# A five-layer transformer stack on one core: GpSimd takes the rounding of a layer's products, a pair of masked keys and a broadcast, and every engine gets a new order

## The reference, cut to what matters

```python
t = t + L2_attn(_ln_t(t))   # 8 heads of 16, causal window of 64
t = t + L2_ffn(_ln_t(t))    # the quantized product, below
t = t + L3_attn(_ln_t(t))   # 8 heads of 16, causal
t = t + L3_ffn(_ln_t(t))    # router, 8 experts of 128x512x128, top 2

def _L2_ffn_ref(x, weight, bias):
    ...
    y = jnp.dot(x, effective_weight) + bias
    act_clipped = jnp.clip(y, -1.0, 1.0)
    quant_dequant = jnp.round(act_clipped * 7.0) / 7.0
    return _ste(y, quant_dequant)      # y + (quant_dequant - y)
```

## Time and profile before

| | |
|---|---|
| median of 3 runs | 240.2 us (240.07 to 240.32) |
| the profiled execution | 240.61 us, span 238.8 us |
| TensorE busy | 227.2 us (95%) |
| VectorE busy | 203.1 us (85%) |
| ScalarE busy | 170.0 us (71%) |
| GpSimd busy | 89.6 us (38%), 155 instructions |
| granted TensorE clock | 0.999 |

### The profile page before, as it was taken

The page is one execution under the profiler, slowest core; times in us unless marked ns, Lnnn a source line. Parts: engine busy times, 40 slices in busy tenths (PEclk is TensorE's granted clock), DMA queues, the critical chain, the costliest instruction groups (busy, mean ns, idle before and its releaser), DMA issues.

```text
span 238.8 us, 4613 instructions
## 1 busy us (share of the span) xinstructions
PE 227.2 (95%) x1493; PEld 172.8 (72%) x1493; DVE 203.1 (85%) x524; ACT 170.0 (71%) x500; POOL 89.6 (38%) x155
## 2 busy tenths in 40 slices
PE   7999999899999999998999979999999999999993
PEld 2588566567876667575876657888888888888882
DVE  2768888975899989999999776999999985899885
ACT  2276454699869986989879968667658766666560
POOL 6200124888864857276733888121100000000000
PEclk9999999999999999999999999999999999999999
DMA  6910000002300200020000333211110004512001
GB/s 187 346 58 4 0 0 0 1 3 88 92 0 5 88 3 0 0 86 6 3 1 0 90 92 96 82 47 44 45 44 0 3 0 116 151 53 78 5 1 44
DMA packets 9319, 11.71 MB, mean 49 GB/s; under 512 B 704, under 2 KB 5952, under 8 KB 9168
## 3 DMA queue, kind: packets, MB, share of 16 engines
q1 hardware_dynamic: 8864, 11.09, 15.4%
q10 hardware_dynamic: 432, 0.33, 0.4%
HBM read 10.87 MB, written 0.56 MB: 48 GB/s over the span
## 4 chain that ended last, share of the span: by engine, by line
PE 76%; DVE 11%; ACT 7%; issue 2%; DMA 1%; POOL 0%; SPq 0%; DVEq 0%; ACTq 0%
PE bank L1317 6%; PE bank L1329 6%; PE bank L1319 6%; PE bank L1318 6%; PE bank L1332 6%; PE bank L1330 6%; PE bank L948 6%; PE bank L924 5%; ACT early_prob L583 4%; PE bank L971 3%; PE bank L882 3%; PE bank L893 2%; ACT prob L583 2%; PE bank L930 2%; PE bank L995 2%
## 5 line engine op out<-in xcount | busy, mean ns | idle before, releaser
L811 ACT ACTIVATE hb<-bank,pk 128x512 f32<-128x512 f32 x64 | 42.9, 705 | 20.7 <-PE bank L1319 20.7
L1818 DVE TENSOR_TENSOR hlo<-hb,hhi 128x512 fp32r<-128x512 f32 x64 | 43.8, 707 | 5.8 <-ACT hhi L814 4.6
L1457 DVE TENSOR_REDUCE negmax<-bank 128x2 f32<-128x384 f32 (+2 forms) x48 | 29.5, 639 | 4.9 <-PE bank L930 4.8
L583 ACT ACTIVATE prob<-bank,negmax 128x192 f32<-128x192 f32 (+1 forms) x64 | 28.9, 508 | 5.1 <-DVE negmax L1457 5.1
L539 ACT ACTIVATE probT<-bank 128x512 f32<-128x512 f32 x38 | 23.1, 638 | 3.4 <-PE bank L948 2.1
L1317 PE MATMUL bank<-xhi,w_hi 128*128 128x512 f32 x64 | 25.3, 396 | 0.0
L1329 PE MATMUL bank<-hhi,w_hi 128*128 128x512 f32 x64 | 25.1, 392 | 0.0
L1319 PE MATMUL bank<-xhi,w_lo 128*128 128x512 f32 x64 | 25.0, 390 | 0.0
L1318 PE MATMUL bank<-xlo,w_hi 128*128 128x512 f32 x64 | 24.9, 390 | 0.0
L1332 PE MATMUL bank<-hlo,w_hi 128*128 128x512 f32 x64 | 24.9, 389 | 0.0
L1330 PE MATMUL bank<-hhi,w_lo 128*128 128x512 f32 x64 | 24.9, 389 | 0.0
(11 more groups left out here) (156 smaller groups left out, 525.9 us busy)
## 6 DMA issues: line engine op xcount, KB each, us to landing
w_raw<-w SPq DMA_DIRECT2D x16, 256.0 KB, 3.1
comb_b<-routes SPq DMA_DIRECT2D x16, 256.0 KB, 3.3
pk<-packed SPq DMA_DIRECT2D x1, 1280.0 KB, 8.9
pk<-packed SPq DMA_DIRECT2D x1, 560.0 KB, 5.9
xs<-x SPq DMA_DIRECT2D x3, 128.0 KB, 2.9
out<-acc SPq DMA_DIRECT2D x3, 128.0 KB, 1.7
xs<-x ACTq DMA_DIRECT2D x1, 128.0 KB, 3.2
out<-acc ACTq DMA_DIRECT2D x1, 128.0 KB, 1.7
```

The lines of the kernel that those rows point to most:

```text
L583: last = nc.scalar.activation(prob_of(n, u)[:, of], lane[n][u % 2][:, of], ACT.Exp, bias=negmax[n][:, unit_query(u), h:h + 1], accum_out=s ...
L811: nc.scalar.activation(hb[blk % 2][:, j, :], h_bank[j][:, :], ACT.Relu, bias=bias).then_inc(h_ready, 1)
L1457: V.tensor_reduce(negmax[n][:, unit_query(u), heads[0]:heads[-1] + 1], lane[n][u % 2][:, :].rearrange("q (h k) -> q h k", h=len(heads))[:, ...
L1818: V.tensor_tensor(hlo[blk % 2][:, j, :], hb[blk % 2][:, j, :], hhi[blk % 2][:, j, :].bitcast(F32), ALU.subtract).then_inc(hlo_ready, 1)
```

## The change

Three pieces of work go from VectorE to GpSimd, with semaphores of their own:

```diff
+            def masked_pair(a, n):
+                pool.wait_ge(k_parts_ready[n % 2], passed(a, n) + 1)
+                for h in unit_heads(n, 2):
+                    last = G.tensor_scalar(kM[n % 2][:, h, :], k_parts[n % 2][:, 0, :].bitcast(F32),
+                                           const("headmask", h, h + 1), 1.0, ALU.mult, ALU.mult)
+                last.then_inc(kM_pair_ready[n % 2], 1)
+            def broadcast_inverse(a, n):
+                pool.wait_ge(rinv_ready[n % 2], passed(a, n) + 1)
+                G.tensor_copy(rb[n % 2][:, :, :, :], rinv[n][:, :, :].unsqueeze(3).to_broadcast([128, TT, HEADS, HD])
+                              ).then_inc(rb_ready[n % 2], 1)
+            def quantize(n):
+                l, done = n % 2, n // 2
+                pool.wait_ge(ffn_copied[l], done + 1)
+                y, z = fy[l], fz[l]
+                G.tensor_scalar(z[:, :, :], y[:, :, :], -1.0, 1.0, ALU.max, ALU.min).then_inc(rounding[l], 1)
+                pool.wait_ge(rounding[l], 2 * done + 1)
+                G.tensor_scalar(z[:, :, :], z[:, :, :], 7.0, ROUND, ALU.mult, ALU.add).then_inc(rounding[l], 1)
+                pool.wait_ge(rounding[l], 2 * done + 2)
+                G.tensor_scalar(z[:, :, :], z[:, :, :], ROUND, 1.0 / 7.0,
+                                ALU.subtract, ALU.mult).then_inc(quantized[l], 1)
...
@@ scores (TensorE)
-                if u in (0, 1):
+                if n % 2 == 0 and u < 2:
+                    pe.wait_ge((kM_ready, kM_pair_ready)[u][n % 2], passed(a, n) + 1)
+                elif u < 2:
                     pe.wait_ge(kM_ready[n % 2], 2 * passed(a, n) + u + 1)
@@ mix (TensorE)
+                    if u == 0:
+                        pe.wait_ge(av_ready[n % 2], p + 1)
@@ inverse_sums (VectorE)
-                step(V.reciprocal(rinv[n][:, :, :], sums[n][:, :, :]))
-                V.tensor_copy(rb[n % 2][:, :, :, :], ...).then_inc(rb_ready[n % 2], 1)
+                V.reciprocal(rinv[n][:, :, :], sums[n][:, :, :]).then_inc(rinv_ready[n % 2], 1)
@@ quantize (VectorE): removed, with its four calls; so are the calls masked_keys(a, n, 1) for n = 0 and 2
```

The orders of all four engines are written anew. On GpSimd, from the third expert's first splits on:

```diff
             split_weights(2, 1)
+            broadcast_inverse(0, 1)
+            broadcast_inverse(0, 0)
+            masked_keys(0, 3)
             masked_keys(0, 2)
-            masked_keys(0, 3)
+            masked_pair(0, 2)
             power(1, 0)
             power(1, 1)
-            after_norm(1, 0)
-            after_norm(1, 1)
-            split_weights(2, 2)
-            split_weights(2, 3)
+            quantize(0)
             add_quantized(0)
+            quantize(1)
+            power(2, 0)
             add_quantized(1)
-            power(2, 0)
             power(2, 1)
             after_norm(2, 0)
             after_norm(2, 1)
+            split_weights(2, 2)
+            split_weights(2, 3)
+            broadcast_inverse(0, 3)
+            broadcast_inverse(0, 2)
+            masked_keys(1, 0)
+            masked_pair(1, 0)
+            masked_keys(1, 1)
...
```

The next pair follows the same pattern. `split_weights(3, 3)` to `(5, 0)` come behind `lower_tokens` of the first pair, then `broadcast_inverse(1, 2)` and `(1, 3)`, then the last eleven pieces, then `power(3, n)` and `lower_tokens` of the second pair. On TensorE, of a middle period (shown: from the second attention's start):

```diff
-            values(1, 0)
-            values(1, 1)
-            scores(1, 1, 0)
-            scores(1, 0, 0)
-            project_out(0, 3)
-            scores(1, 0, 1)
-            project_out(0, 2)
-            scores(1, 1, 1)
-            turn_probs(1, 1, 0)
+            scores(1, 0, 0)
+            values(1, 1)
+            project_out(0, 2)
+            scores(1, 1, 0)
+            project_out(0, 3)
+            values(1, 0)
+            turn_probs(1, 0, 0)
+            scores(1, 0, 1)
+            turn_probs(1, 1, 0)
+            scores(1, 1, 1)
```

More of the change, by code:

```diff
@@ L483, in _ @@
             after_norm(2, 1)
+            split_weights(2, 2)
[5 more added lines that the diff above has]
+            masked_keys(1, 1)
+            power(1, 2)
+            power(1, 3)
+            quantize(2)
+            add_quantized(2)
+            quantize(3)
+            power(2, 2)
+            add_quantized(3)
+            power(2, 3)
+            after_norm(2, 2)
+            after_norm(2, 3)
             split_weights(3, 0)
             split_weights(3, 1)
[L486 to L491, removed]
+            broadcast_inverse(1, 0)
+            broadcast_inverse(1, 1)
+            masked_keys(1, 2)
+            masked_pair(1, 2)
+            masked_keys(1, 3)
+            power(3, 0)
+            power(3, 1)
+            after_norm(3, 0)
+            after_norm(3, 1)
             split_weights(3, 2)
+            for n in PAIRS[0]:
+                lower_tokens(n)
             split_weights(3, 3)
[L494 to L499, removed]
             split_weights(4, 0)
             split_weights(4, 1)
[L502 to L507, removed]
             split_weights(4, 2)
-            for n in PAIRS[0]:
-                lower_tokens(n)
             split_weights(4, 3)
             split_weights(5, 0)
+            for n in PAIRS[1]:
+                broadcast_inverse(1, n)
             split_weights(5, 1)
@@ L1165, in _ @@
             project_out(0, 0)
-            scores(0, 2, 1)
+            project_out(0, 1)
             scores(0, 3, 1)
-            project_out(0, 1)
             turn_probs(0, 2, 0)
-            scores(0, 2, 2)
+            values(0, 2)
             scores(0, 3, 2)
             turn_probs(0, 3, 0)
+            scores(0, 2, 1)
             turn(1, 0)
+            scores(0, 2, 2)
+            scores(0, 3, 3)
+            product(1, 0)
+            mix(0, PAIRS[1], 0)
+            turn(1, 1)
             scores(0, 2, 3)
-            mix(0, PAIRS[1], 0)
-            product(1, 0)
-            turn(1, 1)
-            scores(0, 3, 3)
             turn_probs(0, 2, 1)
             product(1, 1)
+            scores(0, 2, 4)
             scores(0, 3, 4)
-            scores(0, 2, 4)
             turn_probs(0, 2, 2)
@@ L1217, in _ @@
             scores(1, 1, 2)
+            mix(1, PAIRS[0], 0)
+            product(1, 2)
             scores(1, 0, 3)
-            turn_probs(1, 0, 0)
+            scores(1, 1, 3)
+            turn_probs(1, 0, 1)
             turn(1, 3)
-            scores(1, 1, 3)
-            mix(1, PAIRS[0], 0)
+            scores(1, 0, 4)
+            scores(1, 1, 4)
             product(1, 3)
-            turn(1, 2)
-            scores(1, 1, 4)
+            turn_probs(1, 0, 2)
             turn_probs(1, 1, 1)
-            product(1, 2)
@@ L1250, in _ @@
-            project_queries(1, 2)
-            mix(1, PAIRS[0], 4)
             mix(1, PAIRS[0], 5)
+            scores(1, 2, 0)
+            values(1, 3)
+            project_out(1, 0)
+            scores(1, 3, 0)
+            project_out(1, 1)
             values(1, 2)
-            values(1, 3)
-            scores(1, 3, 0)
-            scores(1, 2, 0)
-            project_out(1, 1)
+            turn_probs(1, 2, 0)
             scores(1, 2, 1)
-            project_out(1, 0)
+            turn_probs(1, 3, 0)
@@ L1260, in _ @@
             scores(1, 3, 1)
-            turn_probs(1, 3, 0)
             scores(1, 2, 2)
             scores(1, 3, 2)
+            turn(3, 0)
             scores(1, 2, 3)
-            turn_probs(1, 2, 0)
+            mix(1, PAIRS[1], 0)
+            scores(1, 3, 3)
+            product(3, 0)
             turn(3, 1)
-            scores(1, 3, 3)
-            mix(1, PAIRS[1], 0)
+            turn_probs(1, 2, 1)
+            scores(1, 2, 4)
+            scores(1, 3, 4)
             product(3, 1)
-            turn(3, 0)
@@ L1802, in _ @@
             largest(1, 2, 5)
+            gates(0)
             largest(1, 3, 5)
```

364 lines of the change are left out of this document (172 added, 192 removed).

## The result

Median of 4 runs 245.35 us (245.24 to 245.50), of the kernel before beside it 240.14 us; the ratio is 1.0211, 95% interval 1.0198 to 1.0224. The forecast of 235.8 us was wrong in sign, and the time lies above its range. The profiled execution has a span of 243.7 us (before 238.8), at a granted clock of 1.0.

A forecast was written before the change was run, and what follows sets the result against it. VectorE's queue was taken to bound the attention periods. Gains of 0.5, 2.1, 1.9 and 0.7 by period, less 0.8 behind them, made 4.4 us: median 240.2 to 235.8, own range 233.5 to 237.5, overall 233.0 to 239.6.

The forecast's parts named there:

- what fills them shows in the chain: Attention periods: stalls of 3.1, 3.1 and 3.8 us come from VectorE's queue, which ScalarE's exponentials and TensorE wait for.
- rival 3: Middle periods: gain hidden anyway, as ScalarE's 23.5 and 23.9 us, not VectorE, set them; 240.2 us, chance 0.08.
- TensorE and the loop at 23.3 to 24.0 us: Middle periods: TensorE's work put at 23.3 us, the latency loop through GpSimd's rounding at 24.0, as the next limits.
- rival 4: Middle periods: GpSimd's in-order rounding becomes the loop, deciding from 3.2 us a rounding; slower, 243.3 us or halfway 241.5, chance 0.13.
- Rounding at 1.9 us a sample: GpSimd's quantize: three instructions at about 0.6 us each plus two waits of 0.08; upper bound 2.6.
- Loop closed at S + 24.0: Middle periods: from first scores S, rounding starts at S + 8.0, turn(2, 1) at S + 19.6, then 4.4 us of TensorE.
- rival 2: SBUF contention with GpSimd slows VectorE's remaining instructions by 0.3 us each and TensorE by 1; gain 1.6, 238.6 us, chance 0.08.
- rival 1: GpSimd's clip costs as much as a comparison, 1.3 us; the loop grows to 25.4; 237.7 us, chance 0.17.
- First period +0.5: First attention period: a gain of no more than about 0.5 us, as GpSimd's broadcasts end at about 65.5.
- Fourth period +0.7, gates costed at nothing within 0.7: Last attention period: 22.8 to 22.1 us; gates moved ahead of the last reduction cost nothing, within 0.7.
- Experts' stage -0.8: Behind 143.3 us: GpSimd's late split pieces, nine beside split_hidden, end at about 157; 0.8 us charged.
- Masked pair hidden, broadcasts at 0.5: On GpSimd: the even keys' second masked pair, 1.2 us, is hidden in periods two to four; a broadcast takes 0.5.

The follow-up runs named there:

- addition for subtraction: The changed kernel with the rounding's third GpSimd instruction written as add of -ROUND and multiply instead of subtract and multiply: 243.07 us.
- order alone: The changed kernel with rounding, masked pair and broadcasts back on VectorE, so only the new order and moved splits differ from the kernel before: 241.92 us.
- the version at 252 us: The kernel before, in its own order, with only the four roundings on GpSimd, each right ahead of its add_quantized: 252.35 us.

## Why the prediction was wrong

The step that failed is the first: "what fills them shows in the chain", so VectorE's queue is what the others wait for, and its 4.8 us of relief bring the periods down to the next engines' 24. Relief came (4.0 and 3.5 us, to 20.6 and 21.9 us of VectorE), the periods did not fall but rose by 0.4 and 1.6. The 4.8 took the rounding on VectorE at 1.54 us a sample, 0.72 and 0.53 of it in the two last instructions; in the new order, back on VectorE, these take 0.29 and 0.30. A chain through VectorE shows which engine ended last, not how far behind the next limit lies. In the old order it lay 0.5 us behind in the second period and 0.1 in the third; in the second it was ScalarE, which is rival 3 ("hidden anyway") for that order. The estimate of TensorE and the loop at 23.3 to 24.0 us was of no use as a bound: in the old order, with two engines' work cut, the periods still took 25.3 and 26.0. In the new order the latency decides, rival 4's mechanism, at a lower threshold than its 3.2 us a rounding: already at 2.05 us the second period was no shorter than with the rounding on VectorE.

- *Rounding at 1.9 us a sample.* It took 2.73. The argument that clipping needs no 0/1 result was wrong, and the subtraction, taken for the same as a multiply, was the second slow instruction. Worth 2.3 us of the kernel's time, measured by addition for subtraction for the 0.67 it removes; rival 1 had only the clip's 0.7.
- *Loop closed at S + 24.0.* The product's sum with the bias ended at S + 8.1 as forecast (66.91 to 75.03). The working goes on over `turn(2, 1)`, 11.6 us later; it came 14.2 later (89.20), and the 4.4 us behind it took 4.5 (to 93.73). But the chain closes over the first sample: `turn(2, 0)` waits for a power that stands behind the second rounding in GpSimd's order, and all 8.3 us of TensorE follow it. By the working's own terms it is due 7.5 us behind the sum (1.9 + 2.4 + 1.9 + 0.7 + 0.6). It came 10.4 behind it (85.39): 1.7 of the 2.9 is the two roundings' price, and 1.0 is the norm's two instructions, which took 1.54 us beside GpSimd's add where the second sample's took 0.60; the rest is short waits. What `power(2, 0)` ahead of the second rounding would give was not tested. The longer norm is rival 2's mechanism, once, on the path:

```profile
83.79 1.54 DVE L1462 TENSOR_SCALAR ht<-t,mv,rstd 128x128 f32<-128x128 f32 x2 [2.06 <-POOL rstd L379]
...
87.88 0.60 DVE L1462 TENSOR_SCALAR ht<-t,mv,rstd 128x128 f32<-128x128 f32 x2
```

- *First period +0.5.* It was +0.3 (starts of the second pair compared).
- *Fourth period +0.7, gates costed at nothing within 0.7.* It lost 1.8. The gates cost 1.05 in the period, beyond their bound, and 0.8 net of the experts' stage. The whole loss is already there with order alone (24.83), so it is no matter of the moved work; what beside the gates makes this order slow there, 0.7 us, stays open.
- *Experts' stage -0.8.* It was -1.4. The mechanism is the forecast's: both edits that took pieces out of the stage brought it back. The last piece ended 15.8 us into the stage, where 157 us on the new clock meant 18.9: seven pieces lay beside `split_hidden`, not nine, and still cost more than was charged.
- *Rival 2's sum.* It charges 0.3 for six instructions a period, 1.8 us, but takes that off once for two periods; taken twice the rival comes to 240.4, not 238.6.
- *Masked pair hidden, broadcasts at 0.5.* Right in price, and right that they hide; what they were to bring in the middle periods was nothing, in either order.
- *The SBUF rule* (the Trainium skill, SBUF — State Buffer, section "SBUF: two separate sides": between a GpSimd instruction and a VectorE one in a two-port mode or with two SBUF inputs, whichever starts first holds the shared port pair for the whole instruction). The trace of after agrees in kind: a piece's cast, 0.40 alone, takes 0.74 beside `split_hidden`, and the gates' small instructions, 0.16 to 0.19 when last, 0.67 to 0.73 in three cases ahead of the last reduction, while GpSimd ran pieces.

## What to carry to other kernels

Before moving work off the engine that the chain of waits names, leave that work out and time it: here 1.25 us a sample left out gave 0.9 us of 240, which bounds what a move of just that work can bring in that order. The chain says where to try this, not what it will give. When work moves to a slower engine inside a chain that returns to the next iteration's start, count its latency there, twice if two samples pass in series, over every path that closes the loop, and ask for the duration of the very operation, not of its neighbour in shape. Place background work (here split pieces) in waits whose length the timeline shows, and check what in-order work stands right behind it.

## What the hardware did that was not expected

- GpSimd's time for one instruction form depends on the operation: at 128x256 in fp32, multiply-and-add or add-and-multiply 0.41 us, subtract-and-multiply and maximum-and-minimum 1.08, a multiply by a column 0.47 to 0.50 (0.593 in the kernel before). The Trainium skill, GPSIMD Engine Reference, section 4.1 Engine selection, has one-input work at roughly line rate; the clip's 1.08 against VectorE's 0.284 says otherwise for this operation.
- In the version at 252 us TensorE's granted clock fell after its longest waits. Windows of it: nearly idle, then the clock at its lower level (0.50 is 1.2 GHz) for part of the stretch that follows.

```profile
84.00:88.00 4.00, 0.66 (x4) 0.42 (x4) 0.32 (x3) 2.10 (x10) 3.68 (x6) 1.00 0.00 0
88.00:92.00 4.00, 2.75 (x24) 2.01 (x24) 3.17 (x12) 0.39 (x1) 2.60 (x5) 0.63 0.00 0
...
120.00:124.00 4.00, 1.01 (x5) 1.01 (x6) 3.07 (x11) 0.62 (x3) 2.81 (x5) 0.50 0.00 0
124.00:128.00 4.00, 4.00 (x19) 3.38 (x18) 2.23 (x6) 2.18 (x5) 1.34 (x3) 0.68 0.02 4
```

So a part of its 5.7 and 5.9 us is the slower clock behind the wait, not the wait. In the second period the first five pieces of the chain behind the wait (transposes, a mix, probabilities turned) took 3.7 us there and 2.3 in the kernel before: 1.4 of the 5.7.
